# Message pass of a graph network: three of a group's thirteen one-hot chunks built by ScalarE from absolute distances, ten by VectorE

## The reference, cut to what matters

```
x = _layernorm(x + _L1_gnn_ref(x, edge_index, edge_attr_64, W1, b1, g1, be1, W2, ...))
# in it
h   = concatenate([x[src], edge_attr], 1) @ W1 + b1          # 212500 x 64
h   = (h - mean(h, 0)) * rsqrt(var(h, 0) + eps) * g1 + be1   # batch norm over all edges
msg = h * sigmoid(h)                                         # silu
sums = segment_sum(msg, dst)                                 # this is the message pass
agg = sums / max(count, 1)
```

## Time and profile before

| | |
|---|---|
| median of 3 runs | 8726.93 us (8721.98 to 8735.48) |
| the profiled execution | 8723.48 us |
| its span | 8721.6 us |
| busy in the span | PE 5607.9 us (64%), DVE 2638.1 (30%), ACT 1263.0 (14%), POOL 3565.8 (41%) |
| mean granted clock of TensorE | 0.785 of 2.4 GHz |
| message pass | about 3976 to 4463 us |

### The profile page before, as it was taken

How to read it: one execution, slowest core, us unless ns; L and a number is a source line. 1 busy time by engine, 2 the same in 40 slices (tenths; PEclk the granted TensorE clock), 3 DMA queues, 4 the chain that set the end, 5 groups by cost and what they waited for, 6 DMA issues and landing times.

```text
span 8721.6 us, 167374 instructions
## 1 busy us (share of the span) xinstructions
PE 5607.9 (64%) x64897; PEld 5077.1 (58%) x64897; DVE 2638.1 (30%) x5049; ACT 1263.0 (14%) x1571; POOL 3565.8 (41%) x3541
## 2 busy tenths in 40 slices
PE   6999989965544444446764323333333499999997
PEld 6999779853323223336754323232232499999996
DVE  6999621100000000007863322223232311111002
ACT  4777510000000000003442000000000100000001
POOL 2111000037777777774522777777777100000000
PEclk9999989976666666668985666666666699999996
DMA  4444257753333333333311111111111299898993
GB/s 128 180 183 185 112 172 235 243 144 80 84 79 84 79 81 82 79 83 97 113 51 25 27 27 27 27 27 27 27 27 27 71 291 291 280 290 280 290 291 101
DMA packets 371888, 1095.61 MB, mean 126 GB/s; under 512 B 150990, under 2 KB 154576, under 8 KB 358912
## 3 DMA queue, kind: packets, MB, share of 16 engines
q1 hardware_dynamic: 244416, 924.60, 33.0%
q0 software_dynamic: 108896, 114.33, 6.9%
q10 hardware_dynamic: 18432, 54.53, 1.6%
HBM read 871.53 MB, written 221.62 MB: 125 GB/s over the span
## 4 chain that ended last, share of the span: by engine, by line
POOL 33%; PE 32%; issue 16%; DVE 2%; ACT 2%; DMA 1%; DVEq 0%; POOLq 0%; ACTq 0%; SPq 0%; PEldq 0%
POOL gath L307 33%; PE banks L806 25%; PE banks L325 4%; PE banks L481 1%; PE banks L493 1%; PE banks L473 1%; DVE area L1486 1%; DMA gath<-tab_l,idx 1%; ACT gath L1084 1%; DVE area L523 0%; ACT area L488 0%; PE banks L818 0%; ACT area L1055 0%; PE banks L1219 0%; DMA gath<-counts 0%
## 5 line engine op out<-in xcount | busy, mean ns | idle before, releaser
L307 POOL DMA_INDIRECT gath<-tab_l,idx x3328 | 3139.8, 943 | 2249.7 <-issue 1264.8
L325 PE MATMUL banks<-oneh,gath 128*64 128x128 f32 x6656 | 1042.5, 332 | 1556.3 <-DMA gath<-tab_l,idx 1404.9
L325 PEld LDWEIGHTS banks<-oneh,gath 128*64 128x64 f32 x6656 | 992.5, 174 | 1606.5 <-DMA gath<-tab_l,idx 1466.2
L1227 PE MATMUL banks<-area,ones 128*128 128x448 f32 (+1 forms) x1040 | 680.9, 828 | 1096.6 <-DVE area L1458 1073.8
L1227 PEld LDWEIGHTS banks<-area,ones 128*128 128x128 f32 x1040 | 310.2, 313 | 1427.5 <-issue 1427.0
L806 PE MATMUL banks<-wide,gath 128*128 128x128 f16 x14406 | 846.0, 221 | 34.2 <-DMA gath<-counts 20.1
L806 PEld LDWEIGHTS banks<-wide,gath 128*128 128x128 fp8e4 x14406 | 827.8, 99 | 35.5 <-issue 35.4
L806 PE MATMUL banks<-wide,oneh 128*128 128x128 f16 x14406 | 838.0, 220 | 12.1 <-DVE area L1434 12.1
L806 PEld LDWEIGHTS banks<-wide,oneh 128*128 128x128 fp8e4 x14406 | 820.1, 99 | 12.8 <-issue 12.8
L1458 DVE TENSOR_TENSOR area<-gath,banks 128x448 f32<-128x448 f32 (+1 forms) x256 | 138.8, 584 | 1945.0 <-DMA gath<-tab_l,idx 1945.0
L766 ACT CAST wide<-banks 128x784 uint16<-128x784 f32 x784 | 651.1, 858 | 222.6 <-PE banks L723 222.6
(11 more groups left out here) (209 smaller groups left out, 4923.1 us busy)
## 6 DMA issues: line engine op xcount, KB each, us to landing
gath<-counts SPq DMA_DIRECT2D x392, 784.0 KB, 4.3
oneh<-counts SPq DMA_DIRECT2D x392, 784.0 KB, 4.3
counts<-wide SPq DMA_DIRECT2D x98, 1568.0 KB, 5.2
area<-edge_feat SPq DMA_DIRECT2D x128, 448.0 KB, 4.3
gath<-tab_l,idx POOLq DMA_INDIRECT x3328, 2.4
edge_h<-area ACTq DMA_DIRECT2D x128, 416.0 KB, 5.1
area<-edge_h SPq DMA_DIRECT2D x128, 416.0 KB, 3.2
tab_l<-area SPq DMA_DIRECT2D x28, 224.0 KB, 2.4
```

The costliest lines, as they stand in the source:

```text
L307: pool.indirect_dma_start(out=gath[:, h, c, 0:H], out_offset=None, in_=table[:, :], in_offset=bass.IndirectOffsetOnAxis(ap=idx[:, slot, c: ...
L325: last = T.matmul(window[h][0:width, :], rows_of(h, c), oneh[:, h, c, :], start=(c == 0), stop=(c == C - 1))
L1227: ins = T.matmul(bank[n][:, 0:(hi - lo) * H], ones[:, :], src[:, lo:hi, :].rearrange("p c f -> p (c f)"), start=first and lo == 0, stop=la ...
```

## The change

ScalarE builds the one-hots of the last three chunks (C - CD = 3) of each group; VectorE builds ten. A one-hot element is Relu(1 - |d - n|): exactly 1 where the destination d equals the node number n, and 0 elsewhere, as both are whole numbers. ScalarE copies the group's three destination columns into `group_w`, takes three Abs (one per chunk, as the bias is one column), then one Relu over all three. It reads the node numbers from a second row, `iota_w`, in SBUF, which DVE sets and moves on. The distances go to `apart`, which lies in a buffer that the edge pass has finished with. PE waits for one more semaphore. In the build stage two semaphores become one with doubled counts; the instructions there are the same.

```diff
+CD = 10
+        apart = sta[:, :, 0:(C - CD) * W].rearrange("p s (c w) -> p s c w", w=W)
+        a_hot, a_ready = sem("act_hot_steps"), sem("act_window")
@@ add_windows (VectorE; scale is given in the message pass alone)
+            V.tensor_copy(iota_w[:, 0, :], iota0).then_inc(s_pre, 1)
-            dve.wait_ge(s_pre, 3 * (before + 1))
+            dve.wait_ge(s_pre, 4 * (before + 1))
             dve.sem_inc(p.added, 2)
+            if scale is not None:
+                dve.sem_inc(a_ready, 1)
...
+                        n = C if scale is None else CD
                         ins = V.tensor_tensor(
-                            oneh[:, h, :, :], iota_p.rearrange("p (o w) -> p o w", o=1).to_broadcast([P, C, W]),
-                            dst_f[:, at, :].rearrange("p a (c o) -> p (a c) o", o=1).to_broadcast([P, C, W]),
+                            oneh[:, h, 0:n, :], iota_p.rearrange("p (o w) -> p o w", o=1).to_broadcast([P, n, W]),
+                            dst_f[:, at, 0:n].rearrange("p a (c o) -> p (a c) o", o=1).to_broadcast([P, n, W]),
                             ALU.is_equal)
...
+                if scale is not None:
+                    hold(dve, a_hot, 3 * 2 * ITERS * (w + 1))
+                V.tensor_scalar(iota_w[:, 0, :], iota_w[:, 0, :], float(W), None, ALU.add).then_inc(s_shift, 1)
@@ message loop (ScalarE)
                             q = 2 * (w * ITERS + i) + h
+                            hold(act, a_ready, w + 1)
+                            S.copy(group_w[:, h, 0, CD:C], dst_f[:, bass.ds(2 * i + h, 1), CD:C]
+                                   .rearrange("p a c -> p (a c)")).then_inc(a_hot, 1)
+                            hold(act, a_hot, 3 * q + 1)
+                            for c in range(CD, C):
+                                last = S.activation(apart[:, h, c - CD, :], iota_w[:, 0, :], ACT.Abs, scale=-1.0,
+                                                    bias=group_w[:, h, 0, c:c + 1])
+                            last.then_inc(a_hot, 1)
+                            hold(act, a_hot, 3 * q + 2)
+                            hold(act, p_msg.summed, q + 3)
+                            S.activation(oneh[:, h, CD:C, :], apart[:, h, :, :], ACT.Relu, scale=-1.0, bias=ones[:, 0:1])\
+                                .then_inc(a_hot, 1)
                             hold(act, s_mad, q + 1)
-                            hold(act, p_msg.summed, q + 3)
                             S.activation(gath[:, h, :, 0:H], emsg[:, h, :, :], ACT.Silu).then_inc(s_msg, 1)
@@ message sums (TensorE)
+                def messages(pe, k, h):
+                    hold(pe, a_hot, 3 * (2 * k + h) + 3)
+                    pe.wait_ge(s_msg, 2 * k + h + 3)
+
+                sum_groups(pe, p_msg, n_win, lambda h, c: gath[:, h, c, 0:H], messages)
@@ build stage
-                    V.tensor_tensor(low_oh[u], field(0, P), numbers(P), ALU.is_equal).then_inc(b_low, 1)
-                    dve.wait_ge(b_low, j + 1)
+                    V.tensor_tensor(low_oh[u], field(0, P), numbers(P), ALU.is_equal).then_inc(b_oh, 1)
+                    dve.wait_ge(b_oh, 2 * j + 1)
```

More of the change, by code:

```diff
@@ L232, in gnn_program @@
         b_pre, b_turn, b_ready = sem("b_fields"), sem("b_turned"), sem("b_fields_by_edge")
-        b_low, b_oh, b_mm, b_ev = sem("b_low_onehots"), sem("b_onehots"), sem("b_products"), sem("b_counts")
+        b_oh, b_mm, b_ev = sem("b_onehot_steps"), sem("b_products"), sem("b_counts")
         b_st = sems("b_stored")
@@ L389, in add_windows @@
                 V.tensor_scalar(iota_p, iota_p, float(W), None, ALU.add).then_inc(s_shift, 1)
+                if scale is not None:
+                    hold(dve, a_hot, 3 * 2 * ITERS * (w + 1))
+                V.tensor_scalar(iota_w[:, 0, :], iota_w[:, 0, :], float(W), None, ALU.add).then_inc(s_shift, 1)
                 V.tensor_scalar(base_w[:, :], base_w[:, :], float(W), float(NP), ALU.add, ALU.min)\
                     .then_inc(s_shift, 1)
-                hold(dve, s_shift, 2 * (n_win * before + w + 1))
+                hold(dve, s_shift, 3 * (n_win * before + w + 1))
+                if scale is not None:
+                    dve.sem_inc(a_ready, 1)
             dve.sem_inc(s_pass, 1)
@@ L718, in blocks @@
                 if g == 0:
-                    pe.wait_ge(b_oh, j + 1)
+                    pe.wait_ge(b_oh, 2 * j + 2)
                 wait(pe, b_ev, GRP * j + g - 1)
@@ L1253, in edges_to_sums_pe @@
                 last.then_inc(s_bn, 1)
-                sum_groups(pe, p_msg, n_win, lambda h, c: gath[:, h, c, 0:H],
-                           lambda pe, k, h: pe.wait_ge(s_msg, 2 * k + h + 3))
+                def messages(pe, k, h):
+                    hold(pe, a_hot, 3 * (2 * k + h) + 3)
+                    pe.wait_ge(s_msg, 2 * k + h + 3)
+                sum_groups(pe, p_msg, n_win, lambda h, c: gath[:, h, c, 0:H], messages)
                 open_turns(pe, d_z)
```

## The result

The changed kernel takes 8797.18 us (median of 6 runs, 8792.25 to 8802.74), the kernel before 8726.84 on the same chip (6 runs): 70.3 us more, ratio 1.008, interval 1.0067 to 1.0093. It is slower, on the side and by the mechanism that the prediction gave, and 48 us under its 8845, inside both ranges that it gives, 8763 to 8896 and, with the case of one load, 8724 to 8890. A period is, as in the prediction, the time from one even Silu to the next; a period given for a run is the mean over the pass without the first one.

The account below looks back on a forecast made before the run. A ring of dependences, 7.53 us a period, bounds the kernel; ScalarE replaces it at 8.94. 8723.5 + 90 (ScalarE) + 27 (clock) + 1 (other edits) = 8841.5, median 3.4 above: 8845 us, range 8763 to 8896, with one-load case 8724 to 8890.

Parts of the forecast that it names:

- the case of one load: Rival: one load, ahead of the even Silu; ScalarE's period 7.63 us, +6 us, 8733, between 8720 and 8765; chance 0.16.
- the ring: Message pass: matmuls, VectorE's add and shift, table load, Silu, back to TensorE; 7.53 us, the whole old period, 64 of them.
- The loads: Message loop: even Copy and even Silu each get a table load, odd half none; 128 in place of 64.
- the two ways in: Loop body entered from line 1075's Sqrt or the last Silu; its loads must suit both.
- ScalarE's own period: Message pass: two groups 6.24 us, two loads at 1.31, about 0.08 lost overlap: 8.94 us, +90 us in all.
- The two terms that no row showed: ScalarE's waits on itself per group: 0.16 us Copy to Abs, 0.34 Abs to Relu; bounds 0.05 and 0.34 each.
- TensorE's clock: Message pass: idling 3.05 us a period slows TensorE's clock, at most every second period by 1.14 us; 27 us taken.
- its lower end: 8763 us: self-waits at 0.05, ScalarE's period 8.1 us, no slow clock.
- The removed chunks at nothing: VectorE's one-hot loses 3 of 13 chunks, 0.43 us per group, all hidden by load and Silu: gives nothing.
- The faster one, one load at the head: Rival: one load ahead of Copy, cheap self-waits; ScalarE's period 6.8 us, 45 us faster, 8682; chance 0.06.
- the ring without loads: Message pass: with the load gone, the shortened one-hot joins the ring, 6.5 us a period.

Follow-up runs that it names:

- ScalarE's part alone: Changed kernel, but VectorE makes all thirteen chunks and the Relu writes into its own buffer; 9530.65 us against 9462.66 for the kernel before, ratio 1.0072.
- the run with the load at the head: Changed kernel plus a one-element Silu at the head of the loop body, leaving one load there; 9416.73 us against 9435.9 for the kernel before, ratio 0.998.

## Why the prediction was right

- **The bound and the ring.** Right: the old period was the ring with its load, and ScalarE's own order replaced it. ScalarE's part alone gave the whole loss.
- **The loads.** Right: Copy at the head of the body got one of its own, Silu another, the odd half none. A Silu ahead of the loop removed them all, so it is the two ways in that decide. From the end of the Silu at 4209.63 over the load to the Copy (4210.51 to 4211.82) are 1.31 us, with no drain.
- **ScalarE's own period.** Mechanism right, size off: 8.94 forecast, 8.55 measured, 25 us over 64 periods. The prices of Copy, Abs and Relu held (0.19, 0.39, 0.615 us). The two terms that no row showed were too high: 0.12 to 0.13 and 0.26 us where I had 0.16 and 0.34, 0.22 a period; the other 0.17 are overlaps of 0.1 between ready ACTIVATEs, of which I counted too few.
- **TensorE's clock.** Mechanism right, size off: 27 us forecast, 3 to 5 measured. After 2.64 us of idle the clock did fall, ahead of 30 of the 64 pairs, nearly every second one. But such a pair took 7.2 to 7.6 us, not the 8.44 of a pair that starts slow after 21 us of idle. In the period shown the shift starts 5.39 us after TensorE (4207.71 to 4213.10), before 3.82; that puts the ring 0.21 over ScalarE's period, where I had 1.14. Slow pairs of up to 7.3 us cost nothing: their periods have 8.55.
- **The two sizes together.** The 25 us and the 22 to 24 of the clock are about the 48 us by which the forecast is too high. Both errors point the same way, and the range held them because its lower end took the waits at their shortest and no slow clock.
- **The removed chunks at nothing.** Wrong by itself: alone they gave 13 us, by the traces through the odd half's shift and POOL's multiply. In the changed kernel it made no difference, as ScalarE hid it: with thirteen chunks the period was 8.55 too.
- **The rivals.** The faster one, one load at the head, decides from a period under 7.53; it came out at 7.22 when built, with a tiny Silu that the rival doesn't have. My own price put it at 7.63, so its 6% rested on the same too high self-waits. My figure for the ring without loads, 6.5, left the shift and the multiply out: the trace of before had the sign of it, a shift of 1.22 us in one half and 1.01 in the other.

## What to carry to other kernels

Work given to an idle engine costs its whole serial order, table loads and waits on itself included, not its busy time: here an engine that was 40% busy became the bound. Where a loop has one activation function and is entered with another table, call that function once ahead of the loop; without that, a plain function at the head of the body cost a second load here. Taking the loads off a ring can make a kernel slower: ask which instructions of VectorE and GpSimd will now run side by side, and try keeping one operand of VectorE's in PSUM. And let the wait that ends last be the last in the program.

## What the runs showed of the hardware

- Taking the table load off the ring made the kernel slower, 7.53 to 8.32 us a period; with the shift's row in PSUM the same step made it faster, 7.28 to 6.87. So the load had been keeping shift and multiply apart.
- The exclusion works both ways: in the run with the load at the head POOL's pair of multiplies takes 4.79 us in place of 3.85. It starts at 4602.52, just behind a shift of 1.01 us that began at 4602.50.
- Each further semaphore wait behind the one that ends last cost TensorE about 0.2 us: 0.53, 0.28 and 0.10 us from the one-hot's end to the first matmul, with two, one and none behind it.
